# A second PSUM bank for the turn-one projections: the bank of the router's logits is lent to them

## What is computed

```
x = x + recurrent_attention(layernorm(x))
x = x + position_block(layernorm(x))        # attention, then a mixture of experts
x = x + retention(layernorm(x))
x = x + swiglu(layernorm(x))
```

```
qkv  = ln1(x) @ qkv_weight.T               # 384 columns: 4 groups of 4 q heads, one k, one v, 16 wide
s    = causal softmax(q . k * scale)       # 8 x 8 per position and head
h1   = x + (s @ v) @ proj_weight.T
logits = ln2(h1) @ router_weight           # 8 experts per token
```

## Time and profile before

| | us |
|---|---|
| median of 3 runs | 1664.57 (1662.81 to 1665.43) |
| profiled execution | 1661.74 |
| its span | 1659.9 |
| busy: TensorE / its weight loads | 1549.7 / 1327.2 |
| busy: VectorE / ScalarE / GpSimd | 958.6 / 625.6 / 715.0 |
| position attention, turn 0 | about 561 to 602 |
| turn 1 | about 602 to 656 |
| turns 2 to 5 | about 656 to 797 |

### The profile page before, as it was taken

The page is one execution under the profiler, slowest core; times in us unless marked ns, Lnnn a source line. Parts: engine busy times, 40 slices in busy tenths (PEclk is TensorE's granted clock), DMA queues, the critical chain, the costliest instruction groups (busy, mean ns, idle before and its releaser), DMA issues. The chain is left out here.

```text
span 1659.9 us, 35176 instructions
## 1 busy us (share of the span) xinstructions
PE 1549.7 (93%) x11898; PEld 1327.2 (80%) x11898; DVE 958.6 (58%) x2418; ACT 625.6 (38%) x1870; POOL 715.0 (43%) x840
## 2 busy tenths in 40 slices
PE   8999979999999878777699999997999999999998
PEld 6777768888888646676599999985888888888887
DVE  6555425665656594985745554436565565556553
ACT  3333346555555564446511111112333333333331
POOL 3222234444443386983343333316445454544431
PEclk9999979999999999888699999999999999999999
DMA  8687610000000000031423222211000000001000
GB/s 203 122 163 124 111 36 14 14 14 14 13 13 2 17 26 26 26 102 37 176 78 116 70 71 77 65 51 33 21 29 25 22 28 19 28 19 28 23 8 14
DMA packets 91152, 86.33 MB, mean 52 GB/s; under 512 B 11648, under 2 KB 81216, under 8 KB 90656
## 3 DMA queue, kind: packets, MB, share of 16 engines
q1 hardware_dynamic: 69920, 51.46, 13.1%
q0 software_dynamic: 6480, 17.70, 4.0%
q10 hardware_dynamic: 14640, 15.72, 2.7%
HBM read 45.53 MB, written 22.02 MB: 41 GB/s over the span
## 5 line engine op out<-in xcount | busy, mean ns | idle before, releaser
L717 POOL TENSOR_TENSOR probs<-probs,rs 128x384 f32<-128x384 f32 x128 | 104.8, 826 | 189.8 <-DVE rs L899 188.7
L2119 PE MATMUL n_psS<-f_XT,wgu 128*128 128x128 f32 x1536 | 182.2, 275 | 0.9 <-ACT f_XT L2239 0.8
L2119 PEld LDWEIGHTS n_psS<-f_XT,wgu 128*128 128x128 f32 x1536 | 176.6, 192 | 1.7 <-ACT f_XT L2239 1.6
L1777 POOL DMA_INDIRECT XE<-token_rows,held x71 | 71.3, 1004 | 162.3 <-PE e_psX L1796 146.3
L1806 PE MATMUL e_psH<-e_XT,e_W 128*128 128x128 f32 x1136 | 133.0, 275 | 0.8 <-DVE e_W L1878 0.8
L856 ACT ACTIVATE probs<-psS,nm 128x192 f32<-128x192 f32 x256 | 104.1, 419 | 70.9 <-DVE nm L895 64.6
L1806 PEld LDWEIGHTS e_psH<-e_XT,e_W 128*128 128x128 f32 x1136 | 129.8, 192 | 1.0 <-DVE e_W L1878 1.0
L895 DVE TENSOR_REDUCE nm<-psS 128x2 f32<-128x384 f32 x128 | 68.8, 552 | 106.2 <-PE psS L774 89.8
L1816 PE MATMUL e_psY<-w_experts,e_HT 128*128 x568 | 128.4, 379 | 0.0
L1847 ACT ACTIVATE e_HT<-e_psH 128x512 f32<-128x512 f32 x71 | 42.3, 597 | 215.3 <-PE e_psH L1806 215.3
L447 PE MATMUL psKV<-wkv,XT 128*128 128x384 f32 (+1 forms) x384 | 119.2, 460 | 0.8 <-ACT XT L497 0.8
(11 more groups left out here) (286 smaller groups left out, 3387.6 us busy)
## 6 DMA issues: line engine op xcount, KB each, us to landing
KD<-KV SPq DMA_DIRECT2D x256, 66.0 KB, 2.5
expert_out<-YE ACTq DMA_DIRECT2D x35, 256.0 KB, 2.1
w_experts<-in_w ACTq DMA_DIRECT2D x10, 512.0 KB, 4.5
X<-in_x SPq DMA_DIRECT2D x8, 512.0 KB, 6.4
x_turned<-XT SPq DMA_DIRECT2D x32, 128.0 KB, 2.3
XS<-x_turned SPq DMA_DIRECT2D x8, 512.0 KB, 4.0
token_rows<-o_XN SPq DMA_DIRECT2D x32, 128.0 KB, 1.7
out_x<-X SPq DMA_DIRECT2D x32, 128.0 KB, 1.7
```

Source lines behind the costliest of these rows:

```text
L717: nc.gpsimd.tensor_tensor(probs[:, b.q % 4, :, :], probs[:, b.q % 4, :, :], bc(rs[:, b.q % 4, :].unsqueeze(2), [P, 2, KEYS]), ALU.mult).th ...
L2119: mm = pe.matmul(bank[:, m * P:(m + 1) * P], wgu[:, h, f:f + P], FT[:, h, :], start=(m == 0 and h == 0), stop=(m == HALF - 1 and h == KC - ...
```

## The change

`psL` becomes the first 64 columns of a new tile `psLQ` of 384 columns, which takes its bank. From m = 16 on the projections alternate between `psQ` (m even) and `psLQ` (m odd), and wait for the copy of tile m-2 in place of m-1 (not below 16, so that all early tiles are out). `logits` waits at s = 0 of each group for the last projection's copy. Nothing is added or taken away in arithmetic, copies or transfers.

```
-        psL = k.ps(ctx, "o_psL", [P, S, NE])
+        psLQ = k.ps(ctx, "o_psLQ", [P, QKVW])
+        psL = psLQ[:, 0:S * NE].rearrange("p (s e) -> p s e", e=NE)
...
         def q_bank(m):
-            return (psQ, psH[0], psH[1])[m % 3] if m < EARLY else psQ
+            return (psQ, psH[0], psH[1])[m % 3] if m < EARLY else (psQ, psLQ)[m % 2]
...
             def projected_in(m):
                 pe.wait_ge(qt_evac, (m + 1) * KC)
                 if m >= EARLY:
-                    pe.wait_ge(q_copied, m)
+                    pe.wait_ge(q_copied, max(m - 1, EARLY))
...
             def logits(j, s):
                 pe.wait_ge(t_evac, (j * S + s) * KC + KC + 2 * KC)
                 if s == 0:
                     pe.wait_ge(l_copied, j + 1)
+                    pe.wait_ge(q_copied, NI)
```

## The result

| | before | after |
|---|---|---|
| median, first comparison | 1663.03 us (5 runs) | 1656.24 us (5 runs) |
| ratio, 95% interval | | 0.9949 (0.9934 to 0.9963) |
| profiled execution / its span | 1661.74 / 1659.9 | 1655.46 / 1653.6 |

The change makes the kernel faster, by 6.8 us between the medians. Two later comparisons of the same pair gave 0.9967 (0.9954 to 0.998) and 0.9949 (0.9936 to 0.9963), with medians 6.1 and 7.4 us apart. I had forecast 5.9. The ratio is the comparison's own figure and not the quotient of the two medians (that would be 0.9959 in the table); of the time before, the three ratios make 8.5, 5.5 and 8.5 us, with intervals from about 3 to 11.

The account below looks back on a forecast made before the run. Turn 1 was taken as bound by PE waiting for ACT's copy out of the one projection bank. A shift of 6.0 us less 0.1 for the added wait gave 5.9: 1664.57 to 1658.7 us, range 1654.8 to 1662.3.

Parts of the forecast that it names:

- The clock: PE's slow stretch at 613.9 us in turn 1 may go or only move: taken as 0, range -1.4 to +1.4 us.
- The pair: Two projections in each of steps 0 to 5 of turn 1: gain 0.37 + 0.60 = 0.97 us, 5.8 us over six.
- turns 2 to 5: After turn 1, the earlier start via POOL (5.8 us) and DVE (6.2 us) is kept: 6.0 us, the middle.
- faster: Whole kernel measured below 1661.2 us, a difference of about 0.2% or 3.3 us being tellable; chance 0.79.
- The bound: In turn 1 everybody waits for PE, and PE waits for ACT's copies of the projection, 13 times, 7.3 us.
- Hidden gain: Rival: in turn 1 PE's earlier work only lets it wait elsewhere, so no gain, about 1664.6 us; chance 0.10.
- half-way case: Rival: POOL or DVE takes over in some steps of turn 1, gain about 3 us, 1661.7 us; chance 0.08.
- First projection of a step: In turn 1 it waits only for its input, starting at 635.38 in place of 635.75 in step 4: gain 0.37 us.
- Second projection: In turn 1 it follows the transposes by 0.22 us; start to start 1.59 in place of 2.19 us: gain 0.60.
- The added wait: The wait of `logits` at s = 0 may stand alone on PE's queue, 51 ns four times: 0 to 0.2 us, taken as 0.1.
- Bank against bank: PE writing one bank while ACT reads another in turn 1: taken as 0, up to 0.9 us gain left for the range.
- The slower rival: PE alternating over two banks in turn 1 gets more 1.2 GHz stretches, up to 9.7 us slower, 1674.3 us; chance 0.05.

Follow-up runs that it names:

- e2_bank_only: The new bank used in turn but the old wait for the copy of tile m-1 kept, against the kernel before: 1661.58 against 1662.26 us, ratio 0.9998.

## Where the prediction was wrong, and what it had right

The mechanism stood. What failed is the sum of 5.9 us, through three terms. The clock was put at 0, though a price of 1.4 us was at hand: the slow stretch that went was worth 1.3 us in two traces, and in the third the clock cost about 1.7. The pair was put at 0.97 us, so 6.2 for turn 1: it measured 1.05, 6.7 in all. And the shift was kept whole through turns 2 to 5: 0.8 us of it was lost. The first trace so gives 7.2 us inside the stage. The chance of 0.79 for "faster" went by a limit of 0.2%; the gain, 0.51% by the ratio, is clear of that, but small against a coarser limit such as 2%, by which the two kernels take the same time.

**The bound** was read rightly. With the bank alone the ratio is 0.9998; with the wait moved as well it is 0.9949, 0.9967 and 0.9949. "Hidden gain" is out, and so is its half-way case, since POOL (2.17 us ahead of unit 9) and DVE (2.02 us ahead of turn 2) still wait. The profile puts POOL's waits down to "issue" and not to PE, so that they are for PE was an inference; it is borne out by unit 9 coming 7.6 us sooner. In steps 1 and 2 POOL came close: 0.47 and 0.23 us of idle are left where 3.81 and 1.79 were.

**First projection of a step.** Forecast 0.37, measured 0.43 to 0.46. I took 0.15 us from input to start, the value of the release by the copy; the release by the input takes 0.05. What is late next is L1219, as written.

**Second projection.** Forecast 1.59 us from start to start, measured 1.61; gain 0.58 against 0.60.

**A pair** gave 1.05 us, not 0.97; over six pairs and step 6 that is 6.7 us at the closing exponential, not 6.2. This is the mis-sized term of the sum that each trace repeats.

**Turns 2 to 5** did not keep all of it: 0.8 us was lost, where I had put the middle of two ways out. DVE is released 8.0 us sooner than before and POOL 7.6 (both against turn 1's start), and turn 2 then takes longer: the four `ownS` products take 3.25 us, 2.70 before, and by the first `o_var` of the stage 0.4 us of DVE's lead is gone. Before, they read

```profile
661.16 2.70 DVE L1050 TENSOR_TENSOR ownS<-w_experts 128x256 f32<-128x256 f32 x4
```

POOL works without a gap beside these four in both traces, so that doesn't explain the difference, and the cause stays open. The other 0.4 comes in small steps later.

**The added wait** is there as forecast, an instruction of its own, four times, 0.2 us in all at most:

```profile
L1170 PEldq EVENT_SEMAPHORE  x4: 51/51/51, 679.0 to 779.6; - x4
```

**Bank against bank** was nothing: a projection takes 1.51 to 1.56 us in turn 1, 1.53 before.

**The clock** was set at 0 with 1.4 either way, and here the traces disagree with each other: +1.3 in two of them, about -1.7 in the third (48.1 against 45.1, less the 1.3), which is beyond the 1.4 that I allowed. The slower rival, more stretches at 1.2 GHz over two banks, did not come about as a rule. The bank alone was not slower, and from step 2 on no trace of turn 1 shows one.

Sum for the first trace: 6.7 (the wait) + 1.3 (the stretch) - 0.8 (given back) = 7.2 us inside the stage, of which 0.9 shows as a later start of the stage in that execution, 6.3 in the span. The forecast of 5.9 was 0.2 to 1.5 us under the three differences of medians (6.1, 6.8, 7.4), and just outside the intervals of two of the three ratios, which begin at 6.2 us. The pair explains 0.5 of that, the clock and turns 2 to 5 the rest as far as the traces tell; that turns 2 to 5 took back part of what the other two terms had left out, and so kept 5.9 near the result, is luck. The median itself, 1656.24, was 2.5 us under my 1658.7, but 1.5 of these come from the starting point: before had a median of 1664.57 in its first three runs and of 1663.03 in five. The range held the measured median, though its lower end was wrongly added up: 1658.7 - 2.3 - 1 is 1655.4, not 1654.8.

## What to carry to other kernels

Where two engines hand one buffer back and forth, read three times in the timeline: when the input was ready, when the buffer came free, when the work began. The time by which the buffer comes later than the input, summed over the hand-overs, is what a second buffer gives; here it foretold 6.2 us of the 6.7 that turn 1 gained by it. A bank that is idle in the phase in question costs nothing to lend, and then the next latest event (here the input, L1219) is the next thing to move: issuing it ahead of a copy that it does not need took another 4.7 us off turn 1. For a difference of under 0.5% several traces are needed: single ones of one kernel differed by 3 us in 45 for the clock alone, and a slow stretch in turn 3 moved the stage by about 2.5.

## What was not expected of the hardware

A VectorE product of 128x512, 1.26 to 1.5 us in the other traces, took 5.87 us in one (e2_bank_only), beginning while GpSimd was at its value products and ending 0.9 us after GpSimd's run of products ended. The Trainium skill (SBUF — State Buffer, SBUF: two separate sides) says that a VectorE instruction with two inputs in SBUF, as this one has, and GpSimd share a port pair as an exclusive lock, and that the loser blocks for the whole instruction. The trace agrees in so far as the product ended only when GpSimd fell idle; but by the page it would wait for one GpSimd product, by my estimate 0.6 to 0.9 us as the products of that run took, and it waited out eight. In the traces of before and after the same product met a gapless run too and went through, so why it lost here stays open.

The Trainium skill (TensorE: Matmul & The Clock Gate, HAM oscillation) tells of a kernel in which a second PSUM buffer gave no further gain; here, where the copy stood in front of PE, the second bank together with the moved wait gave 6.7 us in turn 1.

Filling the idle time ahead of a slow stretch of TensorE also need not save its cost. With 22 products at the head of turn 1 the first projection fell from 2.93 to 1.56 us, and in that trace a slow stretch came one step later instead, for 1.6 us; the changed kernel without them had one there too in one trace of three.
